# Identity transposes on TensorE in the opening of an adaptive layer-norm transformer block

## The reference

```
mod = (silu(c) @ wmod).reshape(4, 6, 1, 1024)     # c: 4 x 1024, wmod: 1024 x 6144
sa, ca, ga, sb, cb, gb = mod[:, 0] ... mod[:, 5]
ga, gb = sign * max(|.|, 0.25)
h = layernorm(x) * (1 + ca) + sa
x = x + ga * attention(h, wq, wk, wv, wo)         # 32 query heads, 8 key heads, rope, window 256
h = layernorm(x) * (1 + cb) + sb
x = x + gb * mixture(h, gate_w, lora_A, lora_B)   # top 2 of 8 rank-64 experts
```

## Time and profile before

| | |
|---|---|
| median of 3 runs | 2590.11 us (2588.91 to 2591.88) |
| profiled execution | 2590.0 us, of which 2588.2 us are the span from the first to the last instruction |
| PE busy | 2559.2 us, 99% of the span |
| DVE, ACT, POOL busy | 63%, 45%, 6% |
| first matmul of row 0 | at 12.62 us |
| row 7 lands, the last of the modulation | at 34.69 us |

### The profile page before, as it was taken

The page is one execution under the profiler, slowest core; times in us unless marked ns, Lnnn a source line. Parts: engine busy times, 40 slices in busy tenths (PEclk is TensorE's granted clock), DMA queues, the critical chain, the costliest instruction groups (busy, mean ns, idle before and its releaser), DMA issues.

```text
span 2588.2 us, 39774 instructions
## 1 busy us (share of the span) xinstructions
PE 2559.2 (99%) x12705; PEld 2128.3 (82%) x12705; DVE 1628.9 (63%) x4339; ACT 1161.4 (45%) x2581; POOL 156.4 (6%) x82
## 2 busy tenths in 40 slices
PE   7999999999999999999999999999999999999999
PEld 4888888887888888888888888888888888887887
DVE  7677776666666665556666665556666665556653
ACT  4556665453455443333445543333434443335441
POOL 0211122220000000000000000000000000000122
PEclk9999999999999999999999999999999999999999
DMA  8756676649455553347445554347454556456321
GB/s 339 280 211 239 243 268 244 220 169 361 155 179 194 197 181 123 117 153 296 168 156 186 196 181 154 116 146 291 171 190 184 218 195 225 158 187 253 108 82 57
DMA packets 160659, 504.05 MB, mean 195 GB/s; under 512 B 17393, under 2 KB 43697, under 8 KB 159025
## 3 DMA queue, kind: packets, MB, share of 16 engines
q1 hardware_dynamic: 156096, 486.57, 51.8%
q10 hardware_dynamic: 4464, 16.25, 1.6%
HBM read 381.09 MB, written 121.68 MB: 194 GB/s over the span
## 4 chain that ended last, share of the span: by engine, by line
PE 75%; issue 17%; POOL 3%; DMA 2%; DVE 2%; ACT 1%; ACTq 0%; POOLq 0%; DVEq 0%; SPq 0%
PE bank L743 23%; PE bank L745 23%; PE bank L744 23%; PE bank L815 4%; POOL w_q_lo L699 2%; DMA wm<-in_wmod 1%; POOL w_v_lo L699 1%; PE bank L1844 1%; PE bank L259 1%; PE bank L804 0%; DMA stage<-in_wo 0%; PE bank L805 0%; DMA ga_t<-mod_scratch 0%; PE bank L852 0%; PE bank L1895 0%
## 5 line engine op out<-in xcount | busy, mean ns | idle before, releaser
L743 PE MATMUL bank<-w_o_hi,qo_hi 128*128 128x512 f32 x1024 | 411.0, 401 | 0.1
L745 PE MATMUL bank<-w_o_hi,qo_lo 128*128 128x512 f32 x1024 | 400.2, 391 | 0.0
L743 PE MATMUL bank<-hT_hi,w_q_hi 128*128 128x512 f32 x1024 | 399.8, 390 | 0.2 <-DVE swapped L1190 0.2
L744 PE MATMUL bank<-w_o_lo,qo_hi 128*128 128x512 f32 x1024 | 399.0, 390 | 0.0
L745 PE MATMUL bank<-hT_hi,w_q_lo 128*128 128x512 f32 x1024 | 398.5, 389 | 0.0
L744 PE MATMUL bank<-hT_lo,w_q_hi 128*128 128x512 f32 x1024 | 398.5, 389 | 0.0
L999 ACT ACTIVATE prob<-prob,nbias 128x384 f32<-128x384 f32 (+2 forms) x512 | 273.8, 535 | 135.5 <-DVE nbias L1231 124.8
L1095 ACT ACTIVATE pT_hi<-bank 128x384 fp32r<-128x384 f32 (+2 forms) x512 | 205.8, 409 | 225.6 <-PE bank L815 222.2
L1265 DVE TENSOR_TENSOR pT_lo<-bank,pT_hi 128x384 fp32r<-128x384 f32 (+2 forms) x512 | 229.5, 448 | 87.4 <-ACT pT_hi L1095 73.7
L1213 DVE TENSOR_TENSOR acc<-bank,acc 128x512 f32<-128x512 f32 x256 | 173.7, 689 | 175.1 <-PE bank L745 175.1
L1189 DVE TENSOR_TENSOR rotated<-bank,cos_t 128x512 f32<-128x512 f32 x160 | 110.6, 691 | 266.9 <-ACT swapped L982 265.9
(11 more groups left out here) (245 smaller groups left out, 4547.8 us busy)
## 6 DMA issues: line engine op xcount, KB each, us to landing
w_q_hi<-w_q_hi_scratch SPq DMA_DIRECT2D x96, 512.0 KB, 8.3
w_q_lo<-w_q_lo_scratch SPq DMA_DIRECT2D x96, 512.0 KB, 8.9
w_o_hi<-w_o_hi_scratch SPq DMA_DIRECT2D x96, 512.0 KB, 7.8
w_o_lo<-w_o_lo_scratch SPq DMA_DIRECT2D x96, 512.0 KB, 8.5
stage<-in_wq SPq DMA_DIRECT2D x32, 512.0 KB, 6.9
stage<-in_wo SPq DMA_DIRECT2D x32, 512.0 KB, 5.3
w_q_hi_scratch<-w_q_hi SPq DMA_DIRECT2D x32, 512.0 KB, 6.2
w_q_lo_scratch<-w_q_lo SPq DMA_DIRECT2D x32, 512.0 KB, 7.1
```

The source lines that it names most:

```text
L743: eng.matmul(o, st[0], mv_[0], start=start, stop=False)
L744: eng.matmul(o, st[0], mv_[1], start=False, stop=False)
L745: return eng.matmul(o, st[1], mv_[0], start=False, stop=stop)
```

## The change

A helper `pe_awake` issues `count` transposes of the 128x128 unit matrix into the first 128 columns of bank 0. Nothing reads the result, and nothing waits for it. There are 40 of them after `cT` is ready and before row 0, 5 between rows 0 and 1, and 6 between row 1 and the turn of the first quarter, 51 in all.

```diff
--- before.py
+++ after.py
@@ -310,15 +310,25 @@
             if k == KT - 1:
                 mq.then_inc(s_proj, 1)
 
+        def pe_awake(eng, count):
+
+            for _ in range(count):
+                eng.transpose(bank[0][:, 0:P], ident_t[:], ident_t[:])
+
         def p0_pe(eng):
             eng.wait_ge(s_id, 16)
             eng.wait_ge(s_zero, 1)
             eng.wait_ge(s_sil, 4)
             eng.transpose(bank[1][:, 0:KT * BATCH], c_in[:], ident_t[0:KT * BATCH, 0:KT * BATCH]).then_inc(s_ct, 1)
             eng.wait_ge(s_ctc, 1)
+            pe_awake(eng, 40)
             for q in range(4):
                 pe_open_row(eng, 2 * q)
+                if q == 0:
+                    pe_awake(eng, 5)
                 pe_open_row(eng, 2 * q + 1)
+                if q == 0:
+                    pe_awake(eng, 6)
                 if q:
                     pe_open_chunk(eng, 2 * q - 2)
                 pe_open_turn(eng, q)
```

## The result

| | before | after |
|---|---|---|
| median of 20 runs each | 2590.02 us | 2594.68 us |
| lowest to highest | 2588.4 to 2593.25 | 2591.44 to 2597.3 |
| profiled execution | 2590.0 | 2595.45 |
| its span | 2588.2 | 2593.7 |

The ratio is 1.0016 with an interval of 1.001 to 1.0022: the changed kernel is slower by 4.7 us. The forecast was 2590.0, with a range up to 2593.4, so the time lies outside it.

A forecast was written before the change was run, and what follows sets the result against it. Full transfer engines were taken to bound the opening: 2.2 us saved on PE, all given back at rows 3, 5 and 7, 0 added, so 2590.0 us, no change; range 2587.6 to 2593.4.

The forecast's parts named there:

- Transfers bound the opening, and the gain is handed back at rows 3 and 7: Opening: PE 2.2 us ahead at row 2, given back waiting at row 3 (2.0), row 5 (0.1) and row 7.
- When the clock rises: Opening, 40 transposes before row 0: rise time unknown; they end between 11.0 and 15.2 us, 13.1 taken.
- the two ends that the text kept: The 40 transposes: 4.4 us at the upper clock throughout, ending at 11.0, or 8.6 at the lower, ending at 15.2.
- Rival (b): Opening: clock does not rise for the transposes, PE reaches row 7 late; +4.1 us, 2594.1; chance 0.11.
- Rival (a): Rows 5 to 7: rows 6 and 7 queue earlier, up to 0.9 us comes back, 2589.1; chance 0.16.
- Everything from there on should be the trace of before, instruction by instruction: From row 7, at 34.7 us, to the end: the trace stays unchanged.
- added on the path 0: Sum of the forecast: the 51 added transposes put 0 us on the path.
- The text's own test: Row 7 to the end: a distance changed by more than 1 us means the forecast is wrong, by code placement.
- rival (c): PE's loops behind the opening: 102 more instructions shift code, fetch pauses of at most 6.1 us double, 2596; chance 0.05.

The follow-up runs named there:

- place 0: PE's main part put by a jump at slot 0 of a 256-instruction block: kernel before 2592.81 us (1.001), changed kernel 2592.91 us (1.0009).
- the second and third sets: Eight kernels, before or changed, with PE's code moved by a jump to a fixed slot or by instructions never run; medians 2590.68 to 2595.10 us.

## Why the prediction was wrong

- **Transfers bound the opening, and the gain is handed back at rows 3 and 7:** right. Saved up to row 2 were 1.8 us of the 2.2 forecast; at row 7 nothing of it was left, since the 0.18 us there come from an earlier issue of row 0. Rows 3 and 7 started at 21.06 and 34.56, for 21.27 and 34.70 in the text, by the same shift. Row 6 was issued 1.8 us sooner (19.94 instead of 21.75) and landed 0.8 us later (32.02 instead of 31.24): the moment of issue did not count, as the text had it.
- **When the clock rises:** right in kind. It rose at 12.0 us, between the two ends that the text kept. The end of the 40 transposes was put at 13.1 (bounds 11.0 and 15.2) and came at 13.8; row 0 was done at 14.8 instead of 14.2, and row 1 began 0.6 us behind its landing at 14.77, which cost nothing. Rival (b) did not happen: the 40 took 7.17 us and row 0 behind them 1.06, with only identity transposes between the first and it. By the Trainium skill ("TensorE: Matmul & The Clock Gate", Part 4: PE-mode transpose) the full clock doesn't engage for transposes, as one kernel showed it; this trace disagrees, with the pitch going from 0.213 to 0.110 us at 12.0 us.
- **Rival (a), up to 0.9 us gets through row 7:** none did, the 0.18 us being there before the first transpose.
- **"Everything from there on should be the trace of before, instruction by instruction": this is the step that failed.** On PE it holds to 126 us. In the sum it is the term "added on the path 0": 51 transposes also bring 101 instructions, and a shift of the code by 101, with nothing run, is worth 4.1 us. The text's own test was a distance from row 7 to the end changed by more than 1 us, and that is 5.6 us in the profile (the medians differ by 4.7). It was rival (c), which was given a chance of 0.05 and 6.1 us. That its time of 2596 came near, 1.3 us above the median, is luck: it doubled an idle time by assumption. Rival (b)'s 2594.1 came nearer still, and (b) didn't happen.
- **Why (c) was sized too small.** It was argued down with the share of q8, 0.1% of the transfer engines. That share is as good as the same in all the kernels (52 packets, 0.85 MB before and after) and says nothing of what a packet meets. And the mechanism was put in the wrong place: the text looked for PE pausing for its code. PE didn't pause at 104 us: it was busy for all of 100 to 120 us, before and after. The loads of another queue were late, and the pause came 23 us on, by way of ACT's order, at a wait for DVE that had stood at 0.2 us in all before.
- The Trainium skill ("Runtime: NRT & Kernel Launch", Instruction fetch mechanics) gives blocks of 256 instructions, and the runs bear that out: a shift of 256 leaves the time as it was (1.0003 with the change's own 101 and 155 not run; 0.6 us behind row 7 by the medians with increments), where a shift of 101 costs 4 us. It also says that the cost of crossing a block is mostly hidden. For PE at 104 us that holds, since it was busy throughout; but where the blocks fall was worth 4.1 us of 2591 here.

**Shown:** the loss needs no transpose and no clock, only the place of the code; at equal places, or moved by a whole block, the changed kernel is 0.1 to 1.1 us slower, medians that these runs don't tell from nothing. **Shown for four kernels, as a coincidence in time:** a code packet within the loads goes with late landings. **Open:** how one packet, about 1 us on its queue, makes loads 1.0 to 2.6 us later. That the same collision makes all of the 4.7 us is not shown either: of the 5.6 us of the profiled execution 1.9 is followed here to 132 us and 1.6 is the clock drop; the later steps, as 1.0 us between 400 and 512 and 0.5 near 2510 us, were not traced to their cause. Nor was it tried to move the two loads away from the fetch. Why place 0 costs 3 us without the collision is open too. Whether the change has a small cost of its own, for example by a clock drop in some executions, is below what these runs can tell.

## What to carry to other kernels

Whoever adds or takes away instructions ahead of a long program moves every later piece of code in its block, and with it the moment at which code is fetched; here that is worth 0 to 4 us of 2590, as much as the change in question seemed to cost. Before an effect of that size is put down to an edit, run the edit at two or three places (jumped-over instructions ahead of the first wait cost nothing, if the engine is waiting there anyway), and compare at equal places. And where the transfers are full, PE made faster is PE waiting: cut the stretch at the landings first.

## What the runs showed of the hardware that was not expected

- The place of PE's code decides what its fetches meet. Ten kernels that differ in 51 transposes at most (the kernel before, the changed one, and the eight of the second and third sets) have medians from 2590.0 to 2595.1 us. Which of the later fetches and transfers make up the difference was followed only for the loads of 104 us.
- A semaphore increment is not free on PE: 51 of them, with nothing to wait for, put the turn of `c_in` at 9.03 us instead of 6.05, where it had been waiting for DVE. In the opening 256 put row 7 22.5 us later; some of that is lower clock between them, row 7 itself taking 1.91 us there instead of 1.07.
- Identity transposes alone, with idle time ahead of them, bring the upper clock within the 7.17 us of the forty, at 12.0 us. Without them it came at about 20.4 us in one execution and at 16 in another, with the same opening.
- A short idle can be followed by the lower clock, and need not be. With 0.86 of 2 us busy at 144 to 146 the kernel before kept 1.00; with 0.54 of 2 at 146 to 148 the changed one fell to 0.62 and 0.52. The changed kernel at place 0 fell in the opening, behind a wait of 1.42 us at row 3:

```profile
20.00:22.00 2.00, 0.65 (x8) 0.00 (x0) 1.05 (x2) 1.58 (x3) 0.00 (x0) 1.00 0.97 399
22.00:24.00 2.00, 1.93 (x9) 0.39 (x10) 0.94 (x2) 0.11 (x1) 0.00 (x0) 0.57 1.07 440
24.00:26.00 2.00, 2.00 (x6) 1.58 (x7) 0.09 (x1) 0.49 (x1) 0.00 (x0) 0.57 1.01 422
```

By the clock that is 1.7 us of full speed. Its row 7 came 1.36 us late, but mainly for another reason: SP issued rows 0 and 1 at 8.14 us instead of 6.20, and row 7 landed at 36.06 instead of 34.69. The changed kernel waited 1.34 us at the same row and kept its clock. A kernel that is woken early and then left waiting can lose its clock again.
